# Two loops over the token tiles written out as straight code, in a one-core kernel with retention, local attention and two feed-forward nets

## What is computed

```
x = L0_attn_x
xn = _layernorm(x, axis=-1)
x = x + _L0_attn_ref(xn, ...) + _L0_ffn_ref(xn, ...)

# retention, per head
sim = einsum(q, k) * scale * dmask        # causal, decaying
y = (sim @ v) @ ow.T + ob

# one layer of the second branch, two of them in a row
h = shift_token(x); q, k, v = split(h @ wqkv)
q, k = rotary_xpos(l2norm(q) * qs, l2norm(k) * ks)
x = x + local_attention(q, k, v) @ wo
h = layernorm(shift_token(x)) * lg + lb
a, g = split(h @ w1 + b1)
x = x + (a * gelu(g)) @ w2 + b2
```

## Time and profile before

| what | us |
|---|---|
| median of 3 runs | 1040.29 |
| lowest and highest | 1039.1 and 1043.27 |
| the profiled execution | 1042.24 |
| its span, first to last instruction | 1040.4 |
| PE busy | 885.7 (85%) |
| DVE busy | 704.3 (68%) |
| ACT busy | 661.3 (64%) |
| POOL busy | 623.0 (60%) |

### The profile page before, as it was taken

One profiled execution on the slowest core, in us unless ns is written; L12 is line 12 of the kernel. 1 busy time (PEld: TensorE's weight loads), 2 busy tenths in 40 slices (PEclk: granted clock), 3 DMA queues, 4 the chain that ended last, 5 costly groups with the idle time before them and its releaser, 6 DMA issues.

```text
span 1040.4 us, 27565 instructions
## 1 busy us (share of the span) xinstructions
PE 885.7 (85%) x10836; PEld 593.6 (57%) x10836; DVE 704.3 (68%) x1161; ACT 661.3 (64%) x1291; POOL 623.0 (60%) x491
## 2 busy tenths in 40 slices
PE   1667889889879798798898969999999999999876
PEld 1336666656646556666566645756565655656552
DVE  5865765746656557466576577869696969696833
ACT  0444757837658468376474747868686868677643
POOL 4587675855756647647566566757575756565600
PEclk9989999989999899898899989999999999999997
DMA  9000000000000000000000000000000000000000
GB/s 290 13 1 3 2 3 2 2 4 1 2 3 1 3 2 1 4 1 1 3 1 3 1 2 1 2 1 21 0 20 0 20 0 20 0 20 0 21 22 10
DMA packets 20455, 13.18 MB, mean 13 GB/s; under 512 B 4578, under 2 KB 19596, under 8 KB 20236
## 3 DMA queue, kind: packets, MB, share of 16 engines
q1 hardware_dynamic: 15108, 10.49, 3.3%
q10 hardware_dynamic: 5256, 1.31, 0.7%
HBM read 9.70 MB, written 2.10 MB: 11 GB/s over the span
## 4 chain that ended last, share of the span: by engine, by line
PE 43%; DVE 18%; ACT 10%; issue 10%; POOL 4%; DVEq 1%; ACTq 0%; POOLq 0%
DVE m L717 4%; PE pQK L1133 4%; PE pT L1006 4%; PE pM L1203 3%; PE pS L1064 3%; PE pT L1049 3%; PE pM L1081 3%; PE pQK L1296 3%; PE pS L1038 3%; PE pV L1099 3%; DVE xa L880 2%; POOL rn L360 2%; DVE ss L707 2%; DVE mx L727 2%; DVE aqk L889 1%
## 5 line engine op out<-in xcount | busy, mean ns | idle before, releaser
L360 POOL TENSOR_TENSOR rn<-rn,half_neg 128x16 f32<-128x16 f32 x64 | 187.5, 2929 | 5.3
L358 POOL TENSOR_SCALAR rn<-ss 128x16 f32<-128x16 f32 x64 | 16.3, 254 | 230.1 <-DVE ss L707 228.8
L373 POOL TENSOR_TENSOR m<-m 128x1024 f32<-128x1024 f32 x64 | 150.8, 2356 | 0.0
L1133 PE MATMUL pQK<-wqkv,hT 128*128 128x512 f32 x256 | 124.8, 611 | 3.1 <-DVE m L717 3.1
L380 POOL TENSOR_TENSOR qkn<-m,rn 128x1024 f32<-128x1024 f32 x64 | 123.7, 1933 | 6.1 <-POOL m L373 2.0
L727 DVE TENSOR_REDUCE mx<-pS 128x8 f32<-128x1024 f32 x64 | 78.1, 1220 | 63.7 <-PE pS L1038 63.6
L516 ACT ACTIVATE kT<-pT 128x512 f32<-128x512 f32 x64 | 38.0, 594 | 112.9 <-PE pT L1006 112.6
L1006 PE MATMUL pT<-cst,qkn 128*128 128x128 f32 x512 | 73.5, 290 | 23.1 <-issue 19.1
L556 ACT ACTIVATE sq<-pQK 128x1024 f32<-128x1024 f32 x64 | 65.4, 1022 | 27.8 <-PE pQK L1133 27.6
L707 DVE TENSOR_REDUCE ss<-sq 128x16 f32<-128x1024 f32 x64 | 77.5, 1211 | 7.6 <-ACT sq L556 7.6
L540 ACT ACTIVATE prT<-pT 128x1024 f32<-128x1024 f32 x64 | 65.0, 1016 | 23.7 <-PE pT L1049 23.5
(11 more groups left out here) (168 smaller groups left out, 2077.9 us busy)
## 6 DMA issues: line engine op xcount, KB each, us to landing
x<-in_L_attn_x SPq DMA_DIRECT2D x4, 512.0 KB, 9.1
xs<-in_L_attn_x SPq DMA_DIRECT2D x8, 256.0 KB, 2.8
out<-aqkT SPq DMA_DIRECT2D x8, 256.0 KB, 2.2
wqkv<-in_L_ffn_wqkv SPq DMA_DIRECT2D x2, 768.0 KB, 9.7
tab<-in_k_tab SPq DMA_DIRECT2D x1, 1024.0 KB, 10.3
w<-in_L_ffn_w SPq DMA_DIRECT2D x2, 341.0 KB, 10.3
wo<-in_L_ffn_wo SPq DMA_DIRECT2D x2, 256.0 KB
cst<-in_k_cst ACTq DMA_DIRECT2D x1, 404.5 KB, 3.9
```

What stands on the lines that cost most here:

```text
L360: eng.tensor_tensor(rn[:, k % 2, :], rn[:, k % 2, :], half_neg[:, 0:2 * H], ALU.pow).then_inc(S["rn_done"], 1)
L373: eng.tensor_tensor(m1[:, k % 2, :], m1[:, k % 2, :], m2[:, k % 2, :], ALU.add).then_inc(S["add_done"], 1)
L1133: mm = eng.matmul(pQK[:, g * 512:(g + 1) * 512], hT[:, k, :], wqkv[:, l, g * 512:(g + 1) * 512], start=True, stop=True)
```

## The change

In `run_bodies` the two `Fori` loops become Python loops. Each of the four compute engines gets the twelve bodies one after another as code, with `t` an integer: no jump, no register for an address or a count, and `need_apart` falls back to a plain wait. The order of the work on each engine, the tiles, the semaphores and the operations stay. SyncE's own loop and the short loops of the start (`Fori` over halves and quads) stay.

```diff
             body((0, 1), (0, 0), None)
-            with eng.Fori(2, NT) as t:
+            for t in range(2, NT):
                 body((0, t), (0, t - 1), (0, t - 2))
             body((1, 0), (0, NT - 1), (0, NT - 2))
             body((1, 1), (1, 0), (0, NT - 1))
-            with eng.Fori(2, NT) as t:
+            for t in range(2, NT):
                 body((1, t), (1, t - 1), (1, t - 2))
```

## The result

The changed kernel takes 1004.97 us (median of 4 runs, 1002.26 to 1006.68) against 1040.96 us for the kernel before (4 runs, one more than ahead of the prediction, 1039.1 to 1043.27): a ratio of 0.9648, with a 95% interval of 0.9619 to 0.9677, so 36.0 us less. The forecast was 1012 with a range of 1007 to 1019. Of the profiled executions the spans are 1040.4 and 1004.6 us.

The account below looks back on a forecast made before the run. PE bounds the kernel, stalled by code fetched anew after layer 0's five jumps. Savings of 26.6 (those jumps) + 0.3 (layer-1 jumps) + 1.5 (registers) + 0 (fetch) = 28.4 us turn 1040.29 into 1011.9, said as 1012 us; range 1007 to 1019.

Parts of the forecast that it names:

- the register form: All twelve bodies: loop registers and extra waits go, taken as 1.5 us, between 0.7 and 3.7 us.
- the slow clock in retention: Second clock drop inside layer 0's retention, 277.2 to 280.4 us and 557.1 to 560.4: it stays, no gain counted.
- The bound and the mechanism: PE, busiest at 885.7 of 1040.4 us, stalls 3.65 to 3.94 us at five layer-0 jumps while code is brought again.
- The clock behind the jump: After each layer-0 jump PE runs some 3 us at 0.50 of the clock; without a jump it stays at 1.00.
- The first rival: Layer-0 boundaries: the clock still falls, only 18.9 of the 26.6 us go, about 1020 us; chance 10%.
- The five boundaries: Layer 0's five jumps between passes: removing each saves 5.32 us, 26.6 us in all, the main term.
- the trial of a boundary without a jump: Layer 0's loop end, PE going from (0,7) into (1,0): 5.92 us against 11.16 after a jump, used to size the gain.
- The insides: Layer-0 passes between boundaries: register form costs 0.11 us in three slots, at the lower end 6 x 0.11 = 0.7 us.
- Layer 1: Layer 1's loop: five PE jumps worth 0 to 1.2 us, taken as 0.3; registers there nothing at the lower end.
- The fetch at nothing: PE's layer-1 code: five later passes fetched too, some 18 packets of 16 KB, running ahead of PE, cost 0.
- The slower rival: PE's code block boundaries in layer 1's last five passes: starves for code, up to 67 us, 1079 us; chance 3%.
- the jumps as no cost of their own: At the boundary PE would wait as long for something else; time within 0.5%, about 1039 us; chance 2%.

Follow-up runs that it names:

- the named jump: Kernel before, loops and registers kept, plus one instruction at the head of PE's layer-0 pass naming its jump's target: 1015.2 us, ratio 0.9746.

## Why the prediction was right and wrong

The mechanism was right; three terms of the sum were not. The boundary was sized by one sample (2.4 us too little), the register form at 1.5 us where some 4.4 are found, and the slow clock in retention at nothing, where some 2.5 us went.

**The bound and the mechanism: right.** The five stalls of PE in layer 0 were the cost, and they were waits for the head's code. The experiments with two and three tiles to a loop show it by making layer 1 miss as well, the named jump by taking the stall away with the loop kept, and PE straight alone by giving 30 of the 36 us.

**The clock behind the jump: right.** The pause alone brings it, as the run with 3.63 us pauses shows. The first rival, the clock falling at each boundary anyway, didn't come: none of the six boundaries after has a slow stretch. The second of them, after (busy us of the engines, then the granted clock):

```profile
283.10:286.60 3.50, 3.18 (x44) 1.93 (x44) 2.02 (x5) 2.45 (x6) 3.33 (x3) 1.00 0.00 0
```

**The five boundaries: 26.6 us forecast, 29.0 measured.** The step that failed is the trial of a boundary without a jump, taken as typical from one sample. Its 5.92 us held a pause of its own that I had not looked at. Timeline of PE in the kernel before:

```profile
572.03 0.60 PE L1006 MATMUL pT<-cst,qkn 128*128 128x128 f32 x4 [0.23 <-issue]
```

L1006 is broken after four transposes by a packet border: it stands at the same instruction number modulo 256 (125 by the records) as the two pauses in retention ahead of it. Of the five boundaries after, four are 5.42 us and one 5.95, so 5 x 5.92 - 27.63 = 2.0 us of the 2.4. The other 0.4 is that the sample's pass was itself long: its inside of 59.02 us is 0.08 over the mean of the five before it, five times.

**The insides: some 0.7 us forecast, 4.8 measured.** This is the larger miss, and two terms failed. I took the 25 us after the mark as the measure for the whole body (0.11 us) and wrote that the slow clock in retention "stays". The slots do behave like that: after the change L1133 of slot 2 stands at 25.55 us in every pass, as in the earlier trace rows. Retention behind them doesn't. Third pass, mark and last group, after and then the kernel before, both with 6.8 us of slow clock and no border pause:

```profile
288.99 0.38 PE L1116 MATMUL pM<-cst,hn 128*128 128x128 f32 x2
...
347.66 0.46 PE L1283 MATMUL pS<-m 128*32 128x32 f32 x32 [0.33 <-DVE m L863]
```

```profile
301.07 0.38 PE L1116 MATMUL pM<-cst,hn 128*128 128x128 f32 x2
...
360.08 0.46 PE L1283 MATMUL pS<-m 128*32 128x32 f32 x32 [0.39 <-DVE m L863]
```

The inside of all passes without a border pause (none of over 0.18 us), in the traces in which all four engines have the same form, us:

| slow clock inside | registers | constants |
|---|---|---|
| none | 56.49 to 56.76 | 56.05 to 56.31 |
| 3.4 | 57.93 to 58.14 | 57.47 to 57.89 |
| 6.8 | 58.93 to 59.05 | 58.56 to 58.93 |

Read across, the register form costs 0.2 to 0.4 us a pass, where 0.11 had been measured in the slots; for six passes that is an estimated 2 us. It is that of the other engines: with registers on PE alone a pass without slow clock is 56.15 to 56.21 us. Read down, 6.8 us of slow clock cost 2.5. The kernel before has 27.2 us of it in its six passes and the changed one 20.4, none in the last, so an estimated 2.5 us. The border pauses sum to 2.8 us in both and give nothing. Together that is 4.5 of the 4.8 us. The part of the clock is partly luck: two traces with the same layer-0 code as the changed kernel, those with layer 1 by two and by three, have 27.2 and 30.6 us of slow clock, border pauses of 1.5 and 0.6 us and insides of 349.8 and 350.4 us, against 348.9 here and 353.7 before. So of the three only the registers are the same in each trace; clock and pauses come and go by some 2 us between executions of the same layer-0 code. What decides in which pass the clock falls isn't shown. My range gave it a clause and no number.

**Layer 1: 0.3 us for jumps and up to half of 1.5 for registers forecast, 2.6 measured.** The jump is worth nothing there: PE written out alone leaves 50.39 us. The registers of the other engines are worth 0.4 us a body, more than the upper end (0.3) that I had carried over from the slots of layer 0. So the register term of the sum, 1.5 us for twelve bodies, is mis-sized: by the estimate above and the 2.4 us of layer 1's six bodies it is some 4.4, over even the 3.7 of its upper end.

**The fetch at nothing: right in sum.** 17 packets in 726 to 970 us cost no visible time. In retention some borders do cost, 0.2 to 0.8 us where a dense group is cut, but as much before as after (2.8 us in six passes), so the change added nothing there either.

**The slower rival and the jumps as no cost of their own** are refuted by the same lines. Of the two rules of the Trainium skill that were weighed, that of "Runtime: NRT & Kernel Launch", section Instruction fetch mechanics, a jump waiting for its page, holds where the loop is too long; its window of two pages doesn't hold for PE, where a loop of 3 to 4 packets stays, and one of 7.3 when the jump is named. The same section says that kernels prefer full unrolling where possible, and the 36 us agree.

## What to carry to other kernels

Look at the jump back itself in the trace of a loop: it took here either 0.04 to 0.25 us or 3.3 us and more, and the instruction queue's packets in the loop say which. If the code comes anew each pass, write the loop out, or name the jump (which failed here once the pass was 24 instructions longer); a loop of half the length kept its code. The price of registers differs from one part of a body to the next: measure it on the whole body, not on the part where the busiest engine sets the pace. A wait of some 3 us on PE costs more than itself, because the matmuls behind it run at half the clock; filling one such wait with idle matmuls gave 8 us here, for four lines. And a single undisturbed boundary in the trace is a good control for the mechanism but not for the size: look inside it for pauses of its own, and give the stretch where the clock comes and goes a term in the range.

## What was not expected of the hardware

- Where retention's small matmuls are dense, PE stops at some packet borders, in straight code too: mostly for 0.2 to 1.1 us, and twice, with registers in straight code, for 1.8 and 1.9. Where PE's program is straight, all such stops of over 0.25 us lie at instruction 237 to 239 modulo 256, and two were 3.56 us apart.
- One instruction of 31 ns at the head of a loop kept 7.3 packets of code resident for six passes and took 26 us off, and with a pass longer by 24 instructions all five jumps missed again.
- With the head aligned to a packet, the same loop missed at every second jump, 4.7 to 4.9 us in three of four cases.
- The register form of DVE, ACT and POOL cost 0.2 to 0.4 us a body beside constants, and that of PE nothing that the traces show.
- The slow clock inside retention cost about 1.2 to 1.5 us for 3.4 us of it and 2.5 us for 6.8, read where nothing else differs (56.21, 57.39 to 57.75 and 58.68 us inside).
